# Two best of eight experts with MAX8 and MATCH_REPLACE8 in place of repeated maxima, in a vision tower on one core

## The reference, cut to what matters

```python
def _moe(tokens, router_w, w1, b1, w2, b2):                 # level 1
    logits = tokens @ router_w.T
    probs = jax.nn.softmax(logits, axis=-1)
    rw, re = jax.lax.top_k(probs, TOP_K)                    # TOP_K = 2
    rw = rw / jnp.maximum(rw.sum(-1, keepdims=True), 1e-12)
    combine = jnp.zeros((N, E)).at[jnp.arange(N)[:, None], re].set(rw)
    out = tokens
    for e in range(E):
        h = jax.nn.gelu(tokens @ w1[e] + b1[e], approximate=False)
        out = out + combine[:, e:e + 1] * (h @ w2[e] + b2[e])
    return out

top_vals, top_idx = jax.lax.top_k(logits, K)                # level 2, K = 2
w = jax.nn.softmax(top_vals, axis=-1)
w_full = jnp.einsum('bsk,bske->bse', w, jax.nn.one_hot(top_idx, E))
```

## Time and profile before

| | us |
|---|---|
| median of 3 runs | 165.22 (165.15 to 165.26) |
| the profiled execution: time | 165.65 |
| the profiled execution: span from first to last instruction | 163.9 |
| PE busy (share of the span) | 144.8 (88%) |
| VectorE busy | 102.5 (63%) |
| ScalarE busy | 70.9 (43%) |
| GpSimd busy | 32.9 (20%) |

### The profile page before, as it was taken

The page is one execution under the profiler, slowest core; times in us unless marked ns, Lnnn a source line. Parts: engine busy times, 40 slices in busy tenths (PEclk is TensorE's granted clock), DMA queues, the critical chain, the costliest instruction groups (busy, mean ns, idle before and its releaser), DMA issues.

```text
span 163.9 us, 2882 instructions
## 1 busy us (share of the span) xinstructions
PE 144.8 (88%) x1106; PEld 71.8 (44%) x1119; DVE 102.5 (63%) x290; ACT 70.9 (43%) x134; POOL 32.9 (20%) x84
## 2 busy tenths in 40 slices
PE   6999789999999997988999895899879999999960
PEld 1355346645444352534553311366334555564420
DVE  7415578764549529486498599932858467413981
ACT  3725961675555010365340000625664167367423
POOL 8600000047777000005200001500049100000000
PEclk9999999999999999999999999999999999999996
DMA  5999970000000000000031000000000000000001
GB/s 161 321 426 347 274 300 3 0 4 2 2 4 2 0 0 0 0 4 0 0 57 55 0 0 2 0 4 0 0 0 4 0 0 0 4 0 4 2 0 36
DMA packets 4917, 8.26 MB, mean 50 GB/s; under 512 B 2748, under 2 KB 2876, under 8 KB 4775
## 3 DMA queue, kind: packets, MB, share of 16 engines
q1 hardware_dynamic: 4902, 8.07, 15.2%
HBM read 7.70 MB, written 0.37 MB: 49 GB/s over the span
## 4 chain that ended last, share of the span: by engine, by line
PE 61%; DVE 22%; ACT 6%; DMA 4%; issue 3%; POOL 2%; DVEq 0%; ACTq 0%; POOLq 0%
PE ps L445 10%; PE ps L386 8%; PE ps L432 6%; DVE scores L1292 5%; PE ps L803 5%; PE ps L439 4%; PE ps L393 3%; PE ps L400 3%; DMA k_scratch<-k_parts_tok 2%; PE ps L543 2%; PE ps L551 2%; DVE scores_rest L1311 2%; DMA k_parts_img<-k_scratch 2%; PE ps L414 1%; PE ps L594 1%
## 5 line engine op out<-in xcount | busy, mean ns | idle before, releaser
L386 PE MATMUL ps<-idle_operand 128*128 128x512 bf16 x137 | 38.5, 391 | 6.4 <-DVE scores L1292 1.7
L1102 DVE TENSOR_TENSOR hidden_gated<-hidden,ps 128x576 f32<-128x576 f32 x28 | 19.7, 750 | 10.1 <-PE ps L439 10.0
L865 ACT ACTIVATE hidden<-ps,weights_sb 128x576 f32<-128x576 f32 x28 | 19.4, 737 | 11.8 <-PE ps L432 9.3
L386 PEld LDWEIGHTS ps<-idle_operand 128*128 128x128 bf16 x150 | 12.8, 102 | 21.8 <-issue 4.5
L857 ACT ACT_TABLE_LOAD x16 | 20.5, 1283 | 0.3
L845 ACT ACTIVATE squares<-ps 128x288 f32<-128x288 f32 x8 | 3.3, 410 | 33.3 <-PE ps L445 9.0
L445 PE MATMUL ps<-hidden_gated,weights_sb 128*64 128x288 f32 x112 | 16.3, 418 | 0.0
L301 POOL CAST combine_parts_T<-combine_parts_T 48x288 f32<-48x288 bf16 x3 | 1.3, 419 | 65.4 <-DVE combine_parts_T L1073 65.4
L432 PE MATMUL ps<-h,weights_sb 64*128 64x288 f32 x80 | 13.1, 436 | 0.8 <-ACT hidden L865 0.6
L1041 DVE COPY centred<-ps 128x288 f32<-128x288 f32 x8 | 3.7, 457 | 15.7 <-ACT squares L845 15.7
L1292 DVE TENSOR_REDUCE scores<-ps 128x32 f32<-128x512 f32 (+1 forms) x15 | 8.8, 665 | 2.1 <-PE ps L686 2.1
(11 more groups left out here) (286 smaller groups left out, 231.3 us busy)
## 6 DMA issues: line engine op xcount, KB each, us to landing
patch_sb<-patches SPq DMA_DIRECT2D x6, 288.0 KB, 5.2
weights_sb<-weights SPq DMA_DIRECT2D x1, 1108.0 KB, 9.1
weights_sb<-weights SPq DMA_DIRECT2D x1, 717.0 KB, 15.1
weights_sb<-weights SPq DMA_DIRECT2D x1, 689.0 KB, 13.8
weights_sb<-weights SPq DMA_DIRECT2D x1, 640.0 KB, 7.1
weights_sb<-weights SPq DMA_DIRECT2D x1, 512.0 KB, 12.2
weights_sb<-weights SPq DMA_DIRECT2D x1, 394.0 KB, 13.2
weights_sb<-weights SPq DMA_DIRECT2D x1, 375.5 KB, 6.3
```

What stands on the lines that cost most here:

```text
L386: mm(PS[:, bank, :], idle_in[:, 0:P], idle_in[:, :], start=True, stop=True)
L865: act.activation(HR[:, at % RING, :, :], two(ZA if ch % 2 == 0 else ZB), func, bias=w(f"b1_{n}")[:, ch:ch + 1]).then_inc(S["act_out"], 1)
L1102: dve.tensor_tensor(HG[:, at % GRING, :, :], HR[:, at % RING, :, :], two(GATE_AT[n][ch]), ALU.mult)\
```

## The change

In `top2`, which levels 1 and 2 call once each, the two reductions, the two calls of `top_first` and the five instructions for the gates are replaced. MAX8 sorts the eight logits of each of the six groups, one instruction per group. The difference of places 1 and 0 goes to ScalarE as before. One comparison marks the best expert. Places 2 to 7 of the sorted table are overwritten with 3e30, which no logit equals, and MATCH_REPLACE8, one per group, replaces the two best logits with -3e30; a comparison turns that into -1 at the two best and 0 elsewhere (`kept`). After the tanh, `(first - 0.5) * tanh`, and that less 0.5 times `kept`, give the gates.

```diff
             def top2(n):
 
                 p, k = TT, 2 * NT
-                link(dve.tensor_reduce(m6[0][0:p, :], lg[0:p, :, :], AX, ALU.max))
-                top_first(t8[2], lg, m6[0], t8[1], m6[3], p, k)
-                link(dve.scalar_tensor_tensor(lg[0:p, :, :], t8[2][0:p, :, :], NEG, lg[0:p, :, :], ALU.mult, ALU.add))
-                link(dve.tensor_reduce(m6[4][0:p, :], lg[0:p, :, :], AX, ALU.max))
-                dve.tensor_tensor(m6[1][0:p, :], m6[4][0:p, :], m6[0][0:p, :], ALU.subtract).then_inc(S["exp_in"], 1)
-                top_first(t8[3], lg, m6[4], t8[1], m6[3], p, k)
+                best, kept, first = t8[2], t8[3], t8[1]
+                for i in range(k):
+                    step(dve.max(best[0:p, i, :], lg[0:p, i, :]))
+                sync()
+                dve.tensor_tensor(m6[1][0:p, :], best[0:p, :, 1], best[0:p, :, 0], ALU.subtract).then_inc(S["exp_in"], 1)
+                step(dve.tensor_tensor(t_(first, p, k), t_(lg, p, k), best[0:p, :, 0:1].to_broadcast([p, k, E]),
+                                       ALU.is_equal))
+                link(dve.memset(best[0:p, :, 2:E], -3 * NEG))
+                for i in range(k):
+                    step(dve.match_replace(kept[0:p, i, :], best[0:p, i, :], lg[0:p, i, :], 3 * NEG))
+                sync()
+                link(dve.tensor_scalar(t_(kept, p, k), t_(kept, p, k), 3 * NEG, -1.0, ALU.is_equal, ALU.mult))
                 dve.wait_ge(S["exp_out"], n + 1)
-                step(dve.tensor_scalar(m6[3][0:p, :], m6[2][0:p, :], 0.5, 0.5, ALU.mult, ALU.add))
-                link(dve.tensor_scalar(m6[5][0:p, :], m6[2][0:p, :], -0.5, 0.5, ALU.mult, ALU.add))
-                step(dve.tensor_tensor(t8[3][0:p, :, :], t8[3][0:p, :, :], col(m6[3], p, k), ALU.mult))
-                link(dve.tensor_tensor(t8[2][0:p, :, :], t8[2][0:p, :, :], col(m6[5], p, k), ALU.mult))
-                link(dve.tensor_tensor(comb[0:p, :, :], t8[2][0:p, :, :], t8[3][0:p, :, :], ALU.add))
+                link(dve.scalar_tensor_tensor(t_(first, p, k), t_(first, p, k), -0.5, col(m6[2], p, k), ALU.add, ALU.mult))
+                link(dve.scalar_tensor_tensor(comb[0:p, :, :], t_(first, p, k), -0.5, t_(kept, p, k), ALU.add, ALU.mult))
                 split_gates(n)
```

## The result

The changed kernel takes 164.06 us (median of 6 runs, 163.82 to 164.54) against 165.19 (164.83 to 165.53) for the kernel before: a ratio of 0.9932, 95% interval 0.9912 to 0.9951, or 1.13 us less. The forecast was 164.15. Three executions in the experiments stand far above all others and are left out of the ratios: one of the kernel before (459.34 us), one of e7 (186.84) and the profiled one of e5 (336.77, with a matmul on average about twice as long as in the changed kernel's profile).

A forecast was written before the change was run, and what follows sets the result against it. VectorE's gate work was taken to be on the path before TensorE's transposes in both levels, partly covered by TensorE's issued products. Gains of 0.83 and 0.25 us, 1.08 together, took the 165.22 median to 164.15, range 163.9 to 165.0.

The forecast's parts named there:

- VectorE's own sum: In `top2`, up to the gate split: the new sequence takes 2.58 us against 3.54, gaining 0.96 in each level.
- The wait for tanh: On VectorE before the gate products: no wait for ScalarE's tanh in level 1, none or at most 0.1 us in level 2.
- Level 1's cover: TensorE's fourth product and two idle matmuls ahead of the transposes: these start 0.83 us earlier, bounds 0.62 to 0.96.
- Level 2's cover: TensorE's six products issued ahead: transposes come 0.18 to 0.31 us earlier, taken as 0.25; 0.7 of VectorE's gain becomes idle.
- Behind the transposes: Both levels after the transposes: other inputs are ready in time; later K parts and DRAM transfers shift along, costed at nothing.
- The sum: Whole kernel: 0.83 + 0.25 = 1.08 us less, so the median of 165.22 comes to 164.14, say 164.15.
- C: K parts' four transfers: level 1's gain is given back there, only level 2's 0.25 stays, 164.97 us; chance 0.08.
- Rival A: MAX8s and match pairs: unlinked instructions don't overlap, gates take 4.07 us, 0.53 more per level, 166.3 us; chance 0.07.

The follow-up runs named there:

- e7: Kernel before, with only level 2's sixth product moved behind the transposes: 165.64 us, ratio 1.0026 to the kernel before.
- e5: Changed kernel with three linked 96x48 copies added on VectorE ahead of level 1's gate split: 164.72 us, ratio 0.9964 to the kernel before.
- e8: Changed kernel without the two idle matmuls ahead of level 1's transposes: 163.67 us, ratio 0.9911 to the kernel before.
- e6: Changed kernel with three linked 96x48 copies added on VectorE ahead of level 2's gate split: 164.03 us, ratio 0.9933 to the kernel before.
- e1: Kernel before, with the new gates in level 1 only: 164.35 us, ratio 0.9937 to the kernel before.
- e3: Changed kernel with a wait behind every MAX8 and every MATCH_REPLACE8: 165.98 us, ratio 1.0046 to the kernel before.
- e9: Changed kernel without level 1's idle matmuls and with level 2's sixth product behind the transposes: 163.52 us, ratio 0.9906 to the kernel before.
- e4: Changed kernel with level 2's sixth product issued behind the transposes: 163.62 us, ratio 0.9903 to the kernel before.
- e10: e9 with one comparison against the second best logit replacing memset, MATCH_REPLACE8s and their comparison: 163.16 us, ratio 0.9886 to the kernel before.

## Why the prediction was right

By its steps:

- **VectorE's own sum**: 2.58 us predicted (2.57 with its terms not rounded up), 2.53 and 2.57 measured. MAX8 was right (six in 0.50, 0.515 reckoned), and so were the pairs, 0.135 apart. The memset was the mis-sized term: 0.09 us, not 0.178, though its bounds held it.
- **The wait for tanh**: in level 1 it cost nothing, as predicted. In level 2 I allowed for at most 0.1. The tanh ends at 116.05 and the product starts at 116.15, where in level 1 it came 0.22 behind the start of its predecessor and here 0.25: 0.03 us of wait, under cover.
- **Level 1's cover**: the gain was 0.75, within 0.62 to 0.96, where I took 0.83. The shift of ScalarE's chunks came as argued: from the normalised state to the second idle it is 3.79 instead of 4.01. The mis-sized term is the step from the idle to the transposes. I took the 0.22 between two idles; they start 0.31 behind the last one (72.93 to 73.24), which accounts for the 0.08 between 0.83 and 0.75. Why that step is longer, no run shows. e8, which has no idles, is bound by VectorE instead.
- **Level 2's cover**: 0.25 predicted, 0.25 measured, and e6 shows 0.65 us on VectorE to be free there.
- **Behind the transposes** nothing changed: 6.88 and 9.86 us in both kernels. The stretch with the K parts' transfers, which I had costed at nothing, took 32.57 before and 32.64 after, within what it varies from one execution to the next. C is refuted by e1's time, and e1 has 32.57 there.
- **The sum**: 1.08 predicted, 1.01 by the ways, 1.13 by the times. That the time came within 0.1 of the forecast is partly luck, since the interval of the times, 0.8 to 1.5, couldn't have told 1.01 from 1.4; the steps above are the better evidence.
- **Rival A**, the slower side, was a true mechanism in a kernel that isn't this one: e3 makes it happen and pays 0.81 us over the kernel before, for which I had reckoned 1.06.

What I had not looked into is the profiled execution's 0.43 us over the median. The start of the two profiles differs. In the kernel before, the chain shown opens on GpSimd's memsets, and the first product on `ones` (L543) stands at 4.43:

```profile
3.87 0.52 POOL decay L307
...
4.43 3.31 PE ps L543 x4
```

In the changed kernel's profile it opens on TensorE's own idle matmuls:

```profile
1.17 2.74 PE ps L386 x6
3.91 3.03 PE ps L543 x4
```

The group on `ones` ends at 7.74 and at 6.94, so the 0.8 us between the two profiles arise there, ahead of everything that was changed: 0.52 in its start and 0.28 in its length. They don't enter the forecast, which is a difference of ways. GpSimd is hardly the cause, though the chain names it. The kernel waits there for the third memset alone and for a transfer of weights; the memset of `decay` ends at 4.39 and 4.38 in the two profiles; and in e3 and e9 the same wait, 0.32 and 0.22 us, is put down to the transfer. For the two profiles here neither part is settled.

## What to carry to other kernels

A shortened step on one engine gives back only what the next engine isn't busy through: list what that engine has issued ahead of the handover and compare two end times, here 0.26 us and 0.75 us of cover for the same 1 us. Then move that cover: an order that was right for the long step (e7, 0.22 us worse when changed) is wrong for the short one (e4, 0.41 us better). On rows this short, put independent instructions in a run without waits, and judge small edits by the way between two fixed points in the trace, which repeated to 0.02 us where the times of one kernel scattered by 1.3. Time the parts of a replacement apart: here the MAX8s brought the whole gain, while the match pairs with their memset and comparison cost more than what they replaced. One comparison in their place (e10) took about 1.1 us less, at the price of other gates where the second best logit occurs twice.

## What was new about the hardware

- A wait between two short VectorE instructions cost 0.12 to 0.13 us: MAX8 on 96x8 started 0.07 us apart without and 0.20 us with a wait, at durations of 0.150 and 0.165; a match pair 0.135 and 0.255.
- A memset of 96x36 took 0.09 us, half of any other VectorE instruction of the size here.
- A VectorE instruction that waited for ScalarE started 0.09 us after the end shown for the tanh; TensorE started 0.04 us after VectorE's.
- The two transfers of the K parts through DRAM took 6.48 to 6.99 us together over thirteen profiles.
